# The chain from the reloaded attention rows to the FFN in two halves of 256 rows, BN_AGGR for mean and variance, and a new order

## The chip, the cores and the metric

The kernel runs on one core of a Trainium2 chip. The metric is device time in microseconds (us) of one execution. Engines: PE is TensorE's matmuls, PEld its weight loads, DVE is VectorE, ACT is ScalarE, POOL is GpSimd, SP is SyncE, which issues the DMAs.

## What is computed

A block of attention and a block of FFN, each between layer norms, over x of 4 x 1024 x 512 in float32.

```python
x = L0_attn_x
x = x + _layernorm(_L0_attn_ref(_layernorm(x), ...))
x = x + _layernorm(_L0_ffn_ref(_layernorm(x), ...))

def _L0_attn_ref(x, qkv_w, conv_w0, conv_b0, conv_w1, conv_b1, proj_w, proj_b, ln_w, ln_b):
    tok = x.reshape(B, H * W // C, C)              # tokens of 16 channels
    qkv = (tok @ qkv_w).reshape(B, -1, 3, C)
    ...                                            # two branches, windows of 8 tokens: softmax(q k) v + a 3x3 conv of v
    att = jnp.concatenate([x1, x2], axis=-1) @ proj_w + proj_b
    mu = att.mean(-1, keepdims=True)
    var = ((att - mu) ** 2).mean(-1, keepdims=True)
    tok = tok + (att - mu) * lax.rsqrt(var + EPS) * ln_w + ln_b
    return jnp.transpose(tok, (0, 2, 1)).reshape(B, H, W)

def _L0_ffn_ref(x, w_gate, w_up, w_down, s_gate, s_up, s_down):
    gate = jax.nn.silu((x @ w_gate) * s_gate)      # 512 x 2048, int8 weights
    up = (x @ w_up) * s_up
    return ((gate * up) @ w_down) * s_down         # 2048 x 512
```

## The kernel before

The 4096 rows are worked in 8 tiles of 512. All engines walk one list of named steps, and each engine has code for the steps that concern it, so that an engine's queue is the list cut down to its own steps. `BEFORE` is the preamble: the attention of tile 0 and most of the first half of tile 1's, the casts of the int8 weights, and the chain to the FFN of tile 0. Then comes one body per tile. A body has 48 slots: for each of 16 chunks m a `gate`, an `up` and a `down` slot, three chunks apart for `down` (LAG), and a table (`STEADY`, for the last tile but one `ENDING`) says after which slot each attention or norm step stands. Tile t's body holds the FFN of tile t, the second half of the attention of tile t+1 (p and a in the table) and the first half of that of tile t+2 (b and c); group 0 of a tile is p or b, group 1 is a or c. `STEADY` runs for tiles 0 to 5 (1 to 4 in a hardware loop), `ENDING` for tile 6, `STEADY` once more for tile 7.

The steps of the attention: `ln1_stats`, `ln1_fin`, `ln1_apply` (the first layer norm), `xt` (transposes of normalised rows, TensorE, copied by ScalarE), `qkv` (projection), `qx` (ScalarE copies q into PSUM `ps_x`), `qk` and `pv` (VectorE multiplies 128x2048 products into `prod`, GpSimd halves them into `sum4`), `qk_sum` and `pv_sum` (VectorE reduces), `softmax`, `exp`, `recip`, `attn_out` (GpSimd, in one case of the preamble VectorE), `cat` (transposes), `proj`, `square`, `cent_var`, `cent_std`, `cent_out` (the inner norm; GpSimd scales by `lnw` and adds the tokens into `ratt`). A bank `ps_w[0]` or `ps_w[1]` is handed from one TensorE step to the next once ScalarE or VectorE has read it.

The chain to the FFN: `att_store` (SyncE) writes `ratt` to memory in two parts and reloads it in another layout as `o1` (in the trace, `o`), 2 x 256 rows. `ffn_norm1` (VectorE) takes BN_STATS of the four 128-row blocks of `o1` and `mean_var` makes mean and variance of them with six small operations; GpSimd's `inv_std` makes the inverse deviation (add, power, multiply); `norm1_add` scales `o1` (ScalarE) and adds it to `xr` (VectorE); `ffn_norm2` does the statistics of `xr`, `norm2_apply` (ScalarE) writes the normalised rows into `o1`; `fx` (t, hi, u) transposes them (TensorE), ScalarE rounds them to f16 as `xhi` and VectorE writes the rest as `xlo`. `gate` of chunk 0 waits for the lower 256 rows, `gate` of chunk 8 for the upper ones. `keep_x1` frees `xr` for `load_xr` of the next tile. `finish`, `finish_apply` and `finish_add` are the last norm. In front of the first gate stand matmuls on `ident` without a use for their result (`warm`, `warm_cat`, `warm_fx`).

Of the kernel before, what the change touches and what calls it, by code (L numbers as in the profile page):

```python
# [7 lines left out]
P = 128  # L8
B, H, W = 4, 1024, 512
C = 16  # L10
# [42 lines left out]
def sandwich_kernel(nc, x, qkv_w, conv_w0, conv_b0, conv_w1, conv_b1, proj_w, proj_b, ln_w, ln_b,  # L53
                    w_gate, w_up, w_down, s_gate, s_up, s_down, scratch, out):
    with ExitStack() as ctx:  # L55
# [25 lines left out]
        epsx = sb("epsx", [P, NQ])  # L81
# [128 lines left out]
        f_chain = sem("f_chain")  # L210
        f_stats = sem("f_stats")
        f_pool = sem("f_pool")
        f_rs = sem("f_rs")
# [67 lines left out]
        def body_steps(plan, last=False):  # L281
# [14 lines left out]
            if last:  # L296
# [1101 lines left out]
```

## Time and profile before

| | |
|---|---|
| time, median of 3 runs | 1010.31 us (1009.2 to 1011.27) |
| the profiled execution | 1010.6 us |
| its span, first to last instruction | 1008.9 us |
| PE busy | 909.3 us, 90% of the span |
| DVE busy | 852.0 us, 84% |
| POOL busy | 720.0 us, 71% |
| ACT busy | 624.6 us, 62% |
| mean granted clock of TensorE | 0.959 |
| DMA | 46.14 MB, 46 GB/s on the mean |

The busy time is a mean over stages. The time before the first gate matmul and the bodies have to be read apart. An idle time is put down to the engine whose signal came last. Instructions can overlap: a group's duration may reach beyond the start of the next on the same engine.

### The profile page before, as it was taken

What the parts mean: (1) busy time and instruction counts of PE and PEld (TensorE: products, weight loads), DVE (VectorE), ACT (ScalarE), POOL (GpSimd) and SP (SyncE); (2) the same over time, 40 slices, a digit from 0 to 9 for tenths busy, and PEclk for the clock granted to TensorE, in tenths of its full rate; (3) what the DMA queues carried; (4) which work ended last, traced back from release to release, by engine and by line L of the source; (5) the groups of instructions that cost most, each with busy time, mean ns of one, the idle gap of its engine ahead of it and who ended that gap; (6) DMA issues with size and microseconds to landing.
All of it is one profiled execution on the core that took longest, in us unless ns stands there. A gap on an engine that the chain in (4) does not pass through costs nothing. (4 is left out here: it accounts for less than half of the span.)

```text
span 1008.9 us, 18469 instructions
## 1 busy us (share of the span) xinstructions
PE 909.3 (90%) x6503; PEld 707.5 (70%) x6503; DVE 852.0 (84%) x1270; ACT 624.6 (62%) x1058; POOL 720.0 (71%) x539
## 2 busy tenths in 40 slices
PE   3636628999999999999999999999999999999996
PEld 3424418777777777877777777777787777777773
DVE  6898898899999999999999999999999999353132
ACT  2745826867586767766686758676776665452431
POOL 3656656787779886997789876987699788542332
PEclk9866958999999999999999999999999999999998
DMA  6011050014102320114002310232011301120001
GB/s 179 0 43 42 1 125 1 1 42 114 34 2 64 84 64 0 33 48 111 16 0 62 98 48 0 62 83 62 1 25 53 76 17 63 54 52 2 22 1 42
DMA packets 78319, 46.14 MB, mean 46 GB/s; under 512 B 39608, under 2 KB 72376, under 8 KB 78264
## 3 DMA queue, kind: packets, MB, share of 16 engines
q1 hardware_dynamic: 73400, 45.10, 16.9%
q10 hardware_dynamic: 4864, 0.32, 0.3%
q8 instruction: 33, 0.54, 0.2%
q14 instruction: 22, 0.18, 0.1%
HBM read 28.63 MB, written 16.78 MB: 45 GB/s over the span
## 5 line engine op out<-in xcount | busy, mean ns | idle before, releaser
L1118 DVE TENSOR_TENSOR prod<-ps_x,qkvl 128x2048 f32<-128x2048 f32 x128 | 290.8, 2280 | 10.4 <-ACT ps_x L786 6.5
L650 PE MATMUL ps_gate<-xhi,wg 128*128 128x256 f16 x1024 | 230.6, 273 | 2.3 <-DVE xlo L1229 1.7
L650 PE MATMUL ps_gate<-xlo,wg 128*128 128x256 f16 x1024 | 230.5, 273 | 0.0
L650 PE MATMUL ps_up<-xhi,wu 128*128 128x256 f16 x1024 | 230.5, 273 | 0.0
L650 PE MATMUL ps_up<-xlo,wu 128*128 128x256 f16 x1024 | 230.5, 273 | 0.0
L856 ACT ACTIVATE gact<-ps_gate,sgate 128x256 f32<-128x256 f32 x256 | 106.6, 467 | 157.0 <-PE ps_gate L650 155.4
L1012 POOL TENSOR_TENSOR flo<-fuse,fhi 128x512 f16<-128x512 f32 x128 | 148.4, 1162 | 72.4 <-ACT fhi L862 72.3
L952 POOL TENSOR_TENSOR sum<-prod 128x1024 f32<-128x1024 f32 x64 | 150.6, 2364 | 39.9 <-DVE prod L1118 36.9
L1238 DVE SCALAR_TENSOR_TENSOR fuse<-ps_up,sup,gact 128x256 f32<-128x256 f32 x256 | 110.3, 472 | 75.8 <-PE ps_up L650 63.9
L961 POOL TENSOR_TENSOR sum<-prod 128x1024 f32<-128x1024 f32 x64 | 151.5, 2369 | 19.5 <-DVE prod L1118 12.8
L670 PE MATMUL ps_acc<-wd,flo 128*128 128x512 f16 x512 | 153.3, 379 | 0.0
L670 PE MATMUL ps_acc<-wd,fhi 128*128 128x512 f16 x512 | 153.3, 379 | 0.0
L606 PE MATMUL ps_w<-wqkvl,xt 128*128 128x256 f32 x512 | 135.6, 404 | 18.5 <-ACT xt L768 12.7
L606 PEld LDWEIGHTS ps_w<-wqkvl,xt 128*128 128x128 f32 x512 | 97.9, 202 | 40.1 <-ACT xt L768 16.1
L650 PEld LDWEIGHTS ps_gate<-xhi,wg 128*128 128x128 f16 x1024 | 100.2, 98 | 22.1 <-DVE xlo L1229 1.9
L650 PEld LDWEIGHTS ps_gate<-xlo,wg 128*128 128x128 f16 x1024 | 100.2, 98 | 21.1
L650 PEld LDWEIGHTS ps_up<-xlo,wu 128*128 128x128 f16 x1024 | 100.2, 98 | 13.5
L650 PEld LDWEIGHTS ps_up<-xhi,wu 128*128 128x128 f16 x1024 | 100.7, 98 | 11.6
L777 ACT ACTIVATE qkvl<-ps_w 128x512 f32<-128x512 f32 x128 | 74.8, 595 | 44.3 <-PE ps_w L606 40.5
L670 PEld LDWEIGHTS ps_acc<-wd,flo 128*128 128x128 f16 x512 | 50.1, 98 | 60.4
L1127 DVE TENSOR_REDUCE ps_x<-sum 128x256 f32<-128x1024 f32 x64 | 78.0, 1220 | 15.6 <-POOL sum L952 15.6
L862 ACT ACTIVATE fhi<-fuse 128x512 f16<-128x512 f32 x128 | 80.3, 628 | 1.3 <-DVE fuse L1238 1.3
(155 smaller groups left out, 1411.4 us busy)
## 6 DMA issues: line engine op xcount, KB each, us to landing
xb<-in_L_attn_x SPq DMA_DIRECT2D x64, 128.0 KB, 2.7
xr<-in_L_attn_x SPq DMA_DIRECT2D x16, 512.0 KB
attn_rows<-ratt SPq DMA_DIRECT2D x16, 512.0 KB, 3.5
o<-attn_rows SPq DMA_DIRECT2D x32, 256.0 KB, 4.2
out_x<-y SPq DMA_DIRECT2D x15, 512.0 KB
x<-in_L_ffn_w_gate SPq DMA_DIRECT2D x1, 1024.0 KB, 5.4
xr<-in_L_ffn_w_up SPq DMA_DIRECT2D x1, 1024.0 KB, 8.2
out_x<-y SPq DMA_DIRECT2D x2, 256.0 KB
```

The source lines that it names most:

```text
L606: mm = nc.tensor.matmul(bank.ps[:, 4 * WC * i:4 * WC * i + 4 * WC], xt[:, 2 * wp + i, :], wqkvl[:, br].rearrange("p f x -> p (f x)"), star ...
L650: mm = nc.tensor.matmul(ps[:, HALF * i:HALF * i + HALF], w[:, k, P * j:P * j + P], xs[:, k, rows], start=(k == 0 and part == 0), stop=(k = ...
L670: return nc.tensor.matmul(ps_acc[q][:], f[:, m % SPLITS, HALF * i + P * q:HALF * i + P * q + P], wd[:, 2 * c + i, :], start=(c == 0 and pa ...
L777: nc.scalar.activation(qkvl[:, g, br, :, 2 * wp:2 * wp + 2].rearrange("p f w x -> p w f x"), bank.ps[:].rearrange("p (w f x) -> p w f x", ...
L856: a = nc.scalar.activation(gact[:, m % 2, part], ps_gate[:, part], ACT.Silu, scale=sgate[:, j:j + 1])
L862: nc.scalar.activation(fhi[:, m % SPLITS, :], fuse[:, m % 2, :], ACT.Copy).then_inc(fhi_done, 1)
L952: nc.gpsimd.tensor_tensor(dst.rearrange("p (s c) -> p s c", c=4), s[:, :, 0:4], s[:, :, 4:8], ALU.add).then_inc(half_done, 1)
L961: nc.gpsimd.tensor_tensor(dst.rearrange("p (s j) -> p s j", j=4), s[:, :, 0:4], s[:, :, 4:8], ALU.add).then_inc(half_done, 1)
L1012: nc.gpsimd.tensor_tensor(flo[:, m % SPLITS, :], fuse[:, m % 2, :], fhi[:, m % SPLITS, :], ALU.subtract).then_inc(flo_done, 1)
L1118: nc.vector.tensor_tensor(prod[:, half].rearrange("p (s j k) -> p s j k", j=WIN, k=WIN), left[:, :, None, :].broadcast_to([P, 4 * WIN, WIN ...
L1127: nc.vector.tensor_reduce(dst, sum4[:, u % 2, :].rearrange("p (s c) -> p s c", c=4), AX.X, ALU.add).then_inc(sum_done, 1)
L1238: a = nc.vector.scalar_tensor_tensor(fuse[:, m % 2, part], ps_up[:, part], sup[:, j:j + 1], gact[:, m % 2, part], ALU.mult, ALU.mult)
```

## The change

The chain from `o1` to `fx` is cut in two: `ffn_norm1`, `norm1_add`, `ffn_norm2` and `norm2_apply` now have a step for each 256 rows, with semaphores of their own. Mean and variance come from BN_AGGR (`moments`, with one spare small operation between the wait and the first BN_AGGR), which gives the variance and the mean with its sign, so GpSimd's `row_std` has one operation more, and for the second norm two more. `ln1_stats` keeps `mean_var`. The multiplication by `lnw` is split in two so that the first half of the rows of `ratt` is ready before the second. `keep_x1` also waits for the last addition into `xr`. All three tables are new; `START` is empty and its steps stand in `BEFORE`.

```diff
-        def scale_norm(eng):
-            eng.tensor_tensor(cent[:].rearrange("p h t c -> p (h t) c"), cent[:].rearrange("p h t c -> p (h t) c"),
-                              lnw[:, None, :].broadcast_to([P, WIN * WIN, C]), ALU.mult).then_inc(lnw_chain, 1)
...
+        def scale_and_add(eng, queue, n, g):
...
             for hi in range(2):
                 c = slice(HB * hi, HB * hi + HB)
+                eng.tensor_tensor(rows[:, :, c], rows[:, :, c], lnw[:, None, c].broadcast_to([P, WIN * WIN, HB]),
+                                  ALU.mult).then_inc(lnw_chain, 1)
+                queue.wait_ge(lnw_chain, 2 * n + hi + 1)
                 eng.tensor_tensor(ratt[:, c, :, WIN * g:WIN * g + WIN].rearrange("p c h t -> p h t c"),
                                   cent[:, :, :, c], token[:, :, :, c], ALU.add).then_inc(ratt_done, 1)
...
+            def row_std(rs, nb, mean, var, chain, base, done, scale=None):
+
+                n = rs.shape[1]
+                nc.gpsimd.tensor_tensor(nb, mean, (negx if scale else negone)[:, 0:n], ALU.mult).then_inc(chain, 1)
+                nc.gpsimd.tensor_tensor(rs, var, eps1[:, 0:n], ALU.add).then_inc(chain, 1)
+                pool.wait_ge(chain, base + 2)
+                nc.gpsimd.tensor_tensor(rs, rs, neghalf[:, 0:n], ALU.pow).then_inc(chain, 1)
+                pool.wait_ge(chain, base + 3)
+                a = nc.gpsimd.tensor_tensor(nb, nb, rs, ALU.mult)
+                if scale:
+                    a = nc.gpsimd.tensor_tensor(rs, rs, scale[:, 0:n], ALU.mult)
+                a.then_inc(done, 1)
...
+            def moments(i, rows, st, chain, n, done):
+
+                dve.wait_ge(chain, n)
+                nc.vector.tensor_scalar(spare[:], st[:, rows[0], 1:2], 0.5, None, ALU.mult)
+                for q in rows:
+                    a = nc.vector.bn_aggr(fmv[:, i, q, :], st[:, q, :])
+                a.then_inc(done, 1)
...
+            def ffn_norm1(t, hi, bank):
+
+                dve.wait_ge(s_o1[hi], 32 * (t + 1))
+                row_stats(o1, 0, (2 * hi, 2 * hi + 1), fst, n1_chain, 2 * t + hi + 1, n1_stats)
...
-            def ffn_norm2(t, bank):
-                dve.wait_ge(xr_sum, NQ * t + NQ)
-                row_stats(xr, 1, fst, f_chain, 6 * t + 3, f_stats, XSCALE ** -2)
+            def ffn_norm2(t, hi, bank):
+                dve.wait_ge(xr_sum, NQ * t + 2 * hi + 2)
+                row_stats(xr, 1, (2 * hi, 2 * hi + 1), fst, n2_chain, 2 * t + hi + 1, n2_stats)
...
-                  (35, ("pv_sum", b, 1)), (35, ("token_bias", c)), (35, ("ffn_norm1", 1)), (36, ("pv_sum", b, 2)),
...
-                  (43, ("ffn_norm2", 1)), (43, ("pv_sum", b, 3)), (43, ("attn_out", b)), (44, ("qk", c, 0)),
...
+                  (35, ("ffn_norm1", 1, 0)), (35, ("finish_apply", 0, 0)), (36, ("qkv", c, 0, 2)), (36, ("recip", b)),
...
+                  (42, ("norm2_apply", 1, 0)), (42, ("qkv", c, 1, 2)), (43, ("attn_out", b)), (43, ("pv_sum", b, 2)),
```

In the steady table the slots are: `ffn_norm1` 35, now 35 and 37; `norm1_add` 38, now 38 and 40; `ffn_norm2` 43, now 41 and 46; `norm2_apply` 44, now 42 and slot 2 of the next body; `fx` of the lower half 46, now 44, of the upper half 4 and 8, now 3 and 8; `attn_out` of a 19, now 22, and its `cat` 23, now 24; `load_xr` 22, now 0; `load_xb` 33, now 22; `att_store` 24, now 21. What follows are the queues of single engines, one row per instruction or per run of like ones (a call that takes two passes over float32 is one row here and two records in the trace).

TensorE's queue from the last projection steps of the preamble to the first gate matmul. L724 (now L733) are the matmuls without a use, L640 (L649) the transposes of `fx`, L617 (L626) `cat` of the next tile. Before:

```order
48 L606 MATMUL ps_w<-wqkvl,xt 128x256 x4
49 L724 MATMUL ps_acc<-ident 128x128 x16
50 L640 MATMUL ps_w<-ident,o 128x128 x8
51 L617 MATMUL ps_w<-ident,qkvl 128x128 x4
52 L650 MATMUL ps_gate<-xhi,wg 128x256
```

and now:

```order
47 L733 MATMUL ps_acc<-ident 128x128 x8
48 L615 MATMUL ps_w<-wqkvl,xt 128x256 x4
49 L607 MATMUL ps_w<-ident,xb 128x128 x4
50 L615 MATMUL ps_w<-wqkvl,xt 128x256 x6
51 L649 MATMUL ps_w<-ident,o 128x128 x8
52 L733 MATMUL ps_acc<-ident 128x128 x8
53 L626 MATMUL ps_w<-ident,qkvl 128x128 x4
54 L659 MATMUL ps_gate<-xhi,wg 128x256
```

One of the two warming groups went ahead of the projection steps, the other behind the transposes.

VectorE's queue in the same place, from the additions into `xr` on. L1127 (L1151) is a reduction, L1118 (L1142) a product, L1229 (L1255) writes `xlo`. Before:

```order
147 L1220 TENSOR_TENSOR xr<-o,xr 128x512 x4
148 L1197 BN_STATS fst<-xr 128x6 x4
149 L1071 TENSOR_TENSOR fmv<-fst 128x4
150 L1072 TENSOR_TENSOR fst<-fst 128x4
151 L1073 TENSOR_TENSOR fst<-fst 128x4
152 L1075 TENSOR_SCALAR fmv<-fmv 128x4
153 L1076 SCALAR_TENSOR_TENSOR fst<-fst 128x4
154 L1079 SCALAR_TENSOR_TENSOR fmv<-fst 128x4
155 L1127 TENSOR_REDUCE attn<-sum 128x256
156 L1118 TENSOR_TENSOR prod<-ps_x,qkvl 128x2048 x2
157 L1229 TENSOR_TENSOR xlo<-ps_w,xhi 128x2x256 x2
```

and now:

```order
146 L1246 TENSOR_TENSOR xr<-o,xr 128x512 x4
147 L1227 BN_STATS fst<-xr 128x6 x2
148 L1220 TENSOR_SCALAR spare<-fst 128x1
149 L1222 BN_AGGR fmv<-fst 128x2 x2
150 L1151 TENSOR_REDUCE attn<-sum 128x256
151 L1142 TENSOR_TENSOR prod<-ps_x,qkvl 128x2048
152 L1255 TENSOR_TENSOR xlo<-ps_w,xhi 128x2x256 x2
153 L1227 BN_STATS fst<-xr 128x6 x2
154 L1220 TENSOR_SCALAR spare<-fst 128x1
155 L1222 BN_AGGR fmv<-fst 128x2 x2
156 L1142 TENSOR_TENSOR prod<-ps_x,qkvl 128x2048
```

One product and the statistics of the upper 256 rows went behind `xlo`.

TensorE's queue where the last transposes of tile 0 stand (the second row of four transposes, L598, now L607; L606, now L615, are the projection steps); the load of tile 1's rows waits for these transposes. Before:

```order
18 L606 MATMUL ps_w<-wqkvl,xt 128x256 x2
19 L598 MATMUL ps_w<-ident,xb 128x128 x4
20 L606 MATMUL ps_w<-wqkvl,xt 128x256 x4
21 L598 MATMUL ps_w<-ident,xb 128x128 x4
22 L606 MATMUL ps_w<-wqkvl,xt 128x256 x8
23 L583 MATMUL ps_w<-mv,pair 128x16
```

and now:

```order
18 L615 MATMUL ps_w<-wqkvl,xt 128x256 x4
19 L607 MATMUL ps_w<-ident,xb 128x128 x4
20 L615 MATMUL ps_w<-wqkvl,xt 128x256 x4
21 L607 MATMUL ps_w<-ident,xb 128x128 x4
22 L615 MATMUL ps_w<-wqkvl,xt 128x256 x4
23 L592 MATMUL ps_w<-mv,pair 128x16
```

Two of the four projection steps of the last branch now stand ahead of its second four transposes.

## Rows read from the trace of the kernel before

**Rows 1.** Busy time by stage: stretch, length, then each engine's us (instructions), PEclk, DMA, GB/s.

```profile
28.46:161.72 133.26, 64.25 (x267) 49.00 (x267) 124.17 (x128) 73.32 (x101) 83.87 (x47) 0.72 0.15 40
267.27:377.02 109.75, 109.34 (x808) 85.79 (x806) 104.03 (x151) 77.09 (x132) 90.61 (x66) 1.00 0.19 49
815.55:909.47 93.92, 91.57 (x708) 70.10 (x706) 64.68 (x109) 50.48 (x90) 62.27 (x50) 1.00 0.17 46
```

**Rows 2.** Waits of TensorE, 161.7 to 998 us: us in total, times, longest.

```profile
PE ps_gate L650 <- DVE xlo L1229: 1.7, 1, 1.7
PE ps_w L617 <- POOL qkvl L459: 1.7, 4, 0.4
PE ps_w L627 <- ACT catt L798: 0.6, 1, 0.6
PE ps_gate L650 <- ACT gact L856: 0.6, 1, 0.6
PE ps_w L598 <- ACT xb L761: 0.4, 1, 0.4
```

**Rows 3.** VectorE in order of time, end of the preamble: start, us, what, count.

```profile
139.09 2.28 DVE L1118 TENSOR_TENSOR prod<-ps_x,qkvl 128x2048 f32<-128x2048 f32 x1
141.28 2.46 DVE L1206 BATCH_NORM_STATS2 fst<-o 128x6 f32<-128x512 f32 x4
...
152.12 0.17 DVE L1071 TENSOR_TENSOR fmv<-fst 128x4 f32<-128x4 f32 x1
152.20 0.16 DVE L1072 TENSOR_TENSOR fst<-fst 128x4 f32<-128x4 f32 x1
...
152.47 0.17 DVE L1075 TENSOR_SCALAR fmv<-fmv 128x4 f32<-128x4 f32 x1
...
152.82 1.21 DVE L1127 TENSOR_REDUCE attn<-sum 128x256 f32<-128x1024 f32 x1
...
160.29 1.29 DVE L1229 TENSOR_TENSOR xlo<-ps_w,xhi 128x512 f16<-128x512 f32 x2 [1.86 <-ACT xhi L828]
```

**Rows 4.** Waits of VectorE, 28 to 162 us: us in total, times, longest.

```profile
DVE prod L1118 <- ACT ps_x L786: 6.5, 2, 3.5
DVE prod L1118 <- POOL sum L952: 2.4, 1, 2.4
DVE xlo L1229 <- ACT xhi L828: 1.9, 1, 1.9
DVE xr L1220 <- ACT o L817: 0.5, 1, 0.5
DVE ps_x L1127 <- POOL sum L952: 0.3, 1, 0.3
```

**Rows 5.** TensorE in order of time in the preamble, with the idle time before.

```profile
51.27 1.09 PE L598 MATMUL ps_w<-ident,xb 128*128 128x128 f32 x4 [0.97 <-ACT qkvl L777]
...
152.96 6.23 PE L724 MATMUL ps_acc<-ident 128*128 128x128 f32 x32 [11.01 <-DVE fmv L1079]
159.02 1.04 PE L640 MATMUL ps_w<-ident,o 128*128 128x128 f32 x8
...
161.72 0.27 PE L650 MATMUL ps_gate<-xhi,wg 128*128 128x256 f16 x1
```

**Rows 6.** SyncE's DMA queue, the load of tile 1's rows.

```profile
52.39 6.10 SPq L498 DMA_DIRECT2D xb<-in_L_attn_x  x8
```

**Rows 7.** ScalarE in order of time in the preamble: a cast, and the second norm applied.

```profile
57.15 1.90 ACT L847 ACTIVATE wu<-xr 128x2048 f16<-128x2048 int8 x1
...
154.58 2.93 ACT L823 ACTIVATE o<-xr,frs 128x512 f32<-128x512 f32 x4 [5.77 <-POOL frs L919]
```

**Rows 8.** GpSimd in order of time, the power on two columns, in a body.

```profile
352.18 0.71 POOL L917 TENSOR_TENSOR frs<-frs,neghalf 128x2 f32<-128x2 f32 x1
```

**Rows 9.** VectorE and GpSimd in order of time, behind the last down matmul.

```profile
1000.48 0.16 DVE L1071 TENSOR_TENSOR fmv<-yst 128x1 f32<-128x1 f32 x1
...
1001.31 0.58 POOL L915 TENSOR_TENSOR frs<-fmv,eps 128x1 f32<-128x1 f32 x1 [1.43 <-DVE fmv L1079]
```

More of the change, by code:

```diff
@@ L80, in sandwich_kernel @@
         eps1 = sb("eps1", [P, WIN])
-        epsx = sb("epsx", [P, NQ])
+        negone = sb("negone", [P, NQ])
+        negx = sb("negx", [P, NQ])
+        xscale = sb("xscale", [P, NQ])
+        spare = sb("spare", [P, 1])
         epsc = sb("epsc", [P, 1])
@@ L1189, in cent_out, with row_stats, ffn_norm1, norm1_add @@
                     dve.wait_ge(cn_done, n + 1)
-                    scale_norm(nc.vector)
-                    dve.wait_ge(lnw_chain, n + 1)
                     dve.wait_ge(xl_done, 4 * n + 4)
-                    add_token(nc.vector, g)
-            def row_stats(src, i, st, chain, base, done, scale=1.0, blocks=slice(0, NQ)):
-                for q in range(blocks.start, blocks.stop):
+                    scale_and_add(nc.vector, dve, n, g)
+            def moments(i, rows, st, chain, n, done):
[4 more added lines that the diff above has]
+                a.then_inc(done, 1)
+            def row_stats(src, i, rows, st, chain, n, done):
+                for q in rows:
                     a = nc.vector.bn_stats(st[:, q, :], src[:, q, :])
                 a.then_inc(chain, 1)
-                mean_var(st[:, blocks], W, fmv[:, i, blocks, 0], fmv[:, i, blocks, 1], chain, base, done, -1.0, scale)
-            def ffn_norm1(t, bank):
-                for hi in range(2):
-                    dve.wait_ge(s_o1[hi], 32 * (t + 1))
-                    for q in (2 * hi, 2 * hi + 1):
-                        a = nc.vector.bn_stats(fst[:, q, :], o1[:, q, :])
-                a.then_inc(f_chain, 1)
-                mean_var(fst, W, fmv[:, 0, :, 0], fmv[:, 0, :, 1], f_chain, 6 * t, f_stats, -1.0)
-            def norm1_add(t, bank):
+                moments(i, rows, st, chain, n, done)
+            def ffn_norm1(t, hi, bank):
+                dve.wait_ge(s_o1[hi], 32 * (t + 1))
+                row_stats(o1, 0, (2 * hi, 2 * hi + 1), fst, n1_chain, 2 * t + hi + 1, n1_stats)
+            def norm1_add(t, hi, bank):
                 dve.wait_ge(s_xr, 32 * t + 32)
-                for q in range(NQ):
+                for q in (2 * hi, 2 * hi + 1):
                     dve.wait_ge(o1_scaled, NQ * t + q + 1)
@@ L1261, in finish @@
                 dve.wait_ge(acc_read, NQ * t + 2 * hi + 2)
-                row_stats(y, 2, yst, y_chain, 3 * (2 * t + hi), y_stats, blocks=slice(0, 2))
+                row_stats(y, 2, range(2), yst, y_chain, 2 * t + hi + 1, y_stats)
             nc.vector.memset(ones[:], 1.0).then_inc(wvt_done, 1)
```

250 lines of the change are left out of this document (129 added, 121 removed).

## The prediction

> **What bounds the kernel now.** I read the shares by engine first, then the busy time by stage, then the waits of TensorE and VectorE, and last the queues in order of time around the places that the change touches. TensorE is busy 90% of the span (the table above), but that mean mixes two stages. From 28.46 us to the first gate matmul at 161.72 us TensorE works 64.25 of 133.26 us and VectorE 124.17 [rows 1]: the preamble ends when VectorE and the chain behind it let the first FFN half go. From there TensorE is packed: one pass of the body (267.27 to 377.02) has 109.34 of 109.75 us of matmuls, and VectorE, second, 104.03. The waits of TensorE between 161.7 and 998 us confirm it: 1.7, 1.7, 0.6, 0.6 and a last one of 0.4, together 5.0 us out of 836 [rows 2]. The work that TensorE has behind the first gate is the same in both kernels, so the time after the change is the sum of three things: when the first gate starts, how many of those 5.0 us of waits remain or are added, and the tail behind the last down matmul. All sums are made against the profiled execution, 1010.6 us (span 1008.9), which stands 0.3 us above the median of the runs shown, 1010.31.
>
> **Part 1: the work of VectorE in the preamble.** The steps ahead of the first `xlo` lose one product (`qk` of window group c, unit 1, is now behind it): 139.09 to 141.28, 2.2 us [rows 3]. `ffn_norm2` of the upper 256 rows is behind it too: two of four BN_STATS of 0.62, 1.2 us. The two `mean_var` blocks go: each runs from the first small operation at 152.12 to 152.82, 0.7 us, together 1.4 us. In their place stand three `moments` blocks (one spare operation, two BN_AGGR each). No row shows a BN_AGGR. The nearest from below are the small operations on 128x4 values, 0.16 to 0.17 us long, 0.08 apart without a wait (152.12, 152.20) and 0.2 with one (from 152.20 to 152.47 stand one of each) [rows 3]; the nearest from above is a BN_STATS itself, 0.62. An aggregation reads six numbers, so I take the lower row: a block is 0.1 of wait and three times 0.08, about 0.35 us, three make 1.05. Splitting the multiplication by `lnw` adds about 0.1. Sum: 2.2 + 1.2 + 1.4 - 1.05 - 0.1, so 3.7 us less work.
>
> Here a rule of the Trainium skill speaks against counting so. The rows show small operations that start 0.08 us apart although each lasts 0.16, and 0.2 apart where there is a wait. The page "VectorE: DVE Perf Modes", section "The DRAIN you can't avoid", says that the next operation does not start until the pipe is empty and that a semaphore between two costs nothing extra. By it, as an estimate by that page with the durations of the rows, a block of six would cost about 1.0 us and one of three 0.5, and two of the first for three of the second would save 0.5 us; by the rows they save 0.35. The trace disagrees on both halves of the rule, and its spacing is what I use.
>
> **Part 2: the waits of VectorE in the preamble.** Before, it waits 8.1 us between its first product and the last `xlo`: 3.0 (the other half of the 6.5 lies ahead of that product), 2.4, 1.9, 0.5 and 0.3 [rows 4]. The new order moves them. (a) The load of the next tile's rows is issued when the last transpose of tile 0 is done. Before, that transpose stood ahead of the four projection steps, at 51.27, and the load went out at 52.39 [rows 5, 6]. Now it stands behind two of them, and its bank is free only when ScalarE has copied the second. ScalarE reaches that copy after an exponential (ready near 50), a cast of 1.90 us and five copies of 0.6 [rows 7], with two cold projection steps between: near 58. The eight loads, 6.1 us to issue and 2.7 to land, are in near 67; VectorE wants them at 65. A new wait of 2.0 us. (b) The two waits for ScalarE's `ps_x` copies of tile 1 (3.0, and the 2.4 that stood behind GpSimd) remain: the first shrinks to about 0.9 because VectorE comes later, the second grows to between 2.4 and 4.1, since the transposes of the attention output now stand between projection steps 1 and 2 of that branch and wait for VectorE's own `attn_out`; I take 4.1, as TensorE has idled by then and runs at the lower clock. (c) The end of the chain: with the FFN rows in halves, TensorE can transpose the lower half after two of ScalarE's applications, which it could before as well; the wait for `xhi` stays at 2.0. With 0.2 for the later `scale_pow2` the sum is 0.2 + 2.0 + 0.9 + 4.1 + 2.0, about 9.2 us against 8.1. So VectorE is done with the last `xlo` 3.7 - 1.1 = 2.6 us earlier, at 158.9 instead of 161.5.
>
> **Part 3: TensorE's queue ahead of the gate.** Before, 32 warming matmuls (16 calls, two records each) run from 152.96 for 6.2 us, and the transposes start at 159.02 only because these are in front: the first two applications, half of the 2.93 us of four [rows 7], were ready at 156.1. Now one warming group is far ahead and the other, 16 records, stands behind the transposes. The transposes start when VectorE's statistics of the lower half, GpSimd's five small operations (the power on two columns is 0.71 [rows 8], the whole about 1.6) and two applications (1.4) are through: about 155.4 by the walk above. TensorE is cold by then: eight transposes 1.8 to 2.0 us (four took 1.09 at 51.27, eight 1.04 at 159.02), sixteen warming records 1.8 to 3.5 (half of the 6.2 us row and about what is left of it at the upper level), `cat` 0.5. The first gate starts between 159.5 and 161.4; I take 160.0, 1.7 us earlier. The granted clock of that stretch was 0.72 on the mean [rows 1], that is, between its two levels 1.2 and 2.4 GHz. So the warming group, not `xlo`, is last there, and it eats 1 us of the gain.
>
> **Part 4: the body.** The cover of every edit in it is TensorE's packed queue; what can be lost is lost only where VectorE, GpSimd or ScalarE comes late to it. VectorE: four `mean_var` of 0.7 to 0.8 go (3.1 us), six `moments` of 0.35 come (2.1): 104.0 becomes 103.0. GpSimd: four chains of three become six of four or five, 90.6 plus about 3; neither reaches 109.3. In order of slots: `fx` moves from slot 46 to 44, so that 6.6 us of TensorE's work lie between it and the next gate instead of 3.1, and its own input, `norm2_apply` of two rows, must be ready two slots earlier; the chain for it starts two slots earlier and is half as long. Laying VectorE's queue against TensorE's slots with the same durations leaves 1.0 us there, but only 0.2 to 0.5 us at two fuse steps: in a pass without waits TensorE starts the `up` of chunk 11 at 77.4 us, and the fuse of chunk 10 is done at 76.9; from there VectorE has `finish` 3.0, a reduction 1.1, a sum 0.6, a product 2.2 and the next fuse 0.8, done at 84.6, where the `up` of chunk 12 wants it at 84.8. The transposes of `cat` move one slot back while `attn_out` moves three back; its 0.4 us wait in each of four passes stays or goes. SyncE: `load_xr` now stands ahead of the output store and waits for `keep_x1`; the store is queued behind it, some 20 us before `y` is wanted again. The load of `xb` moves ahead eleven slots but behind the reloads, and lands over 15 us early. Both cost nothing. Sum for the body: 0, with a lower bound of -3.3 (all the waits of [rows 2] but the 1.7 on `xlo` go) and an upper of +1.2 in each of six passes.
>
> In the last pass with attention (815.55 to 909.47) the chain to the last tile's first gate ends late: `xlo` holds TensorE for 1.7 us, the largest wait in [rows 2]. Now the lower half goes through in front of the upper, and by the same walk `xlo` is ready 3 us before the gate, although `cent_out` comes some 4 us later in that pass. The 1.7 us go.
>
> **Part 5: the tail.** `mean_var` on one column takes from 1000.48 to GpSimd's start at 1001.31, 0.8 us [rows 9]; now 0.35 plus 0.1 for GpSimd's fourth operation. 0.4 us less.
>
> **Sum:** 1.7 + 0 + 1.7 + 0.4 = 3.8 us. 1010.6 - 3.8 = 1006.8 in the profiled execution, 1006.5 as a median.
>
> **The rivals.** (A) *VectorE becomes the bound of the body.* It works 104 of 109.8 us and its other 5.5 are mostly waits for GpSimd, which its queue order makes. If a BN_AGGR costs 0.4 us instead of 0.08 (it would have to be closer to BN_STATS' 0.62 than to a small operation), the six blocks cost 6 us instead of 2.1, VectorE needs 107, and with its waits 109.4 is passed; or the 0.2 us left at slot 35 isn't there. Either gives about 1.2 us in each of six passes: 1006.5 + 7, 1013.5. It decides from a block cost of about 0.9 us, or from 0.2 us of lateness. For it speaks the thin slack, against it that a wait of TensorE gives VectorE time to catch up. (B) *Nothing comes of the preamble.* If the load of the next tile's rows and the cold projection steps cost 2 us more than I gave them, and the last pass gains but the body gives back its 1.7, the result is 1009.5: within 0.2%. (C) *The waits of the preamble vanish.* If the 2.0 and 4.1 us of part 2 don't show (ScalarE's queue keeps up and TensorE is warm), the first gate starts near 155.5 and the time is 1002.
>
> **How the numbers follow.** Forecast 0.55 (1004 to 1009), A 0.17, B 0.18, C 0.10. A change of 0.2%, 2 us, is about what a measurement of this kernel can tell from none. The forecast lies on the faster side of 1008.3 in nine of ten of its cases: faster 0.50 + 0.10 = 0.60; same 0.05 + 0.18 and 0.01 of A, 0.24; slower 0.16. The range runs from 1002.0 (C) to 1012.0, which leaves out the worse half of A and the better half of C.
>
> **What would show it.** The first gate matmul near 160, with warming matmuls right ahead of it; a wait of VectorE on the BN_STATS of `xb` near 65 us; BN_AGGR rows of 0.16 us; no wait of TensorE on `xlo` at the last tile; waits of TensorE in a body pass of at most 0.5 us. A gate later than 161.5, passes longer than 110.5 us, or BN_AGGR of 0.4 us would prove the forecast wrong.

## The result

The changed kernel takes 1013.76 us in the median (1012.49 to 1015.58), 1.0037 times the kernel before, with a 95% interval of 1.0028 to 1.0047. That is 3.4 us slower, where 3.8 us faster was forecast, and above the upper end of the range, 1012.0. The profiled execution took 1013.88 us, its span is 1011.8.

Busy time of each engine in the kernel after, from its profile page:

```profile
PE 913.4 (90%) x6503; PEld 708.9 (70%) x6503; DVE 840.3 (83%) x1218; ACT 621.4 (61%) x1060; POOL 748.4 (74%) x669
```

VectorE has 12 us less to do than before, GpSimd 28 us more, and neither decides. Busy time by stage, in the columns of [rows 1]: preamble, a steady pass, the pass of `ENDING`:

```profile
28.46:162.09 133.63, 67.75 (x270) 52.66 (x271) 122.74 (x128) 72.66 (x100) 87.29 (x58) 0.69 0.15 40
268.15:378.96 110.81, 109.73 (x807) 85.48 (x806) 103.54 (x146) 76.19 (x132) 94.33 (x82) 1.00 0.18 49
821.35:912.51 91.16, 91.16 (x705) 69.90 (x704) 64.45 (x102) 52.56 (x91) 62.79 (x68) 1.00 0.18 47
```

With the start of each tile's first gate matmul the time splits with no more than rounding left over (the last tile of before begins at 909.24; the window in [rows 1] was drawn a little further):

| | before | after | difference |
|---|---|---|---|
| start to first gate | 161.72 | 162.09 | +0.37 |
| pass 0 | 105.55 | 106.06 | +0.51 |
| passes 1 to 5 | 548.28 | 553.20 | +4.92 |
| pass 6 (`ENDING`) | 93.69 | 91.16 | -2.53 |
| pass 7, to the last down matmul | 89.75 | 89.74 | 0.0 |
| tail | 9.9 | 9.6 | -0.3 |
| span | 1008.9 | 1011.8 | +2.9 |

The loss stands in the steady passes. TensorE's waits from 161.9 to 1002 us, to be laid beside [rows 2]:

```profile
PE ps_w L649 <- ACT qkvl L786: 5.7, 12, 0.6
PE ps_up L659 <- DVE fuse L1264: 0.2, 1, 0.2
```

All waits of before are gone, the 1.7 us on `xlo` and the four on `cat` among them. In their place stand twelve at L649, the transposes of `fx`, two in each of six passes. In order of time in one pass, TensorE:

```profile
365.86 1.03 PE L615 MATMUL ps_w<-wqkvl,xt 128*128 128x256 f32 x4
...
370.63 0.59 PE L679 MATMUL ps_acc<-wd,flo 128*128 128x512 f16 x2
371.81 0.66 PE L649 MATMUL ps_w<-ident,o 128*128 128x128 f32 x4 [0.59 <-ACT qkvl L786]
372.81 0.66 PE L649 MATMUL ps_w<-ident,o 128*128 128x128 f32 x4 [0.35 <-ACT qkvl L786]
```

The idle time is counted from the modelled end of a matmul. What a wait costs is read from start to start: two down matmuls are passed on in 0.43 us, so the first transposes could have started at 371.06 and are 0.75 late; the second come 1.00 behind the first, where four transposes need 0.44: 0.56 late. Together 1.31 us a pass, for 0.94 of idle time. The pass of before that had no wait in the list took 109.22 us; with 1.31 that is 110.53, and the passes of after take 110.6. The `cat` wait of before, 0.4 us of idle, cost 0.5 in the same way (109.75).

That 110.53 comes so close is in part chance, for there is one more loss that the list is too coarse to show. The matmuls of a projection step are passed on in 0.86 us where nothing waits (365.86 to 366.72). In front of the `up` of chunk 12 it is 1.15, so that `up` starts 0.29 us late, with 0.13 us of idle time put down to VectorE's fuse; it is so in each of passes 1 to 5:

```profile
573.27 1.03 PE L615 MATMUL ps_w<-wqkvl,xt 128*128 128x256 f32 x4
574.42 0.28 PE L659 MATMUL ps_up<-xhi,wu 128*128 128x256 f16 x1
```

The 109.22 us of before hold small delays too, 0.2 us together, at other places. ScalarE in the same stretch:

```profile
369.76 1.52 ACT L832 ACTIVATE o<-xr,frs 128x512 f32<-128x512 f32 x2 [2.86 <-POOL frs L946]
371.18 0.58 ACT L786 ACTIVATE qkvl<-ps_w 128x512 f32<-128x512 f32 x1
371.66 0.62 ACT L871 ACTIVATE fhi<-fuse 128x512 f16<-128x512 f32 x1
372.18 0.58 ACT L786 ACTIVATE qkvl<-ps_w 128x512 f32<-128x512 f32 x1
```

`norm2_apply` (L832) stands ahead of the copies of two projection steps, the first of which TensorE had finished near 366.9 (its four matmuls from 365.86). ScalarE waits 2.86 us for GpSimd's inverse deviation with that copy behind it, and the two banks that `fx` is to use stay full. GpSimd is late because VectorE's statistics are done only at 366.9; GpSimd is then on a long addition that lasts to 367.1, a `flo` stands next in its queue, and the five small operations start behind that:

```profile
366.66 0.24 DVE L1222 BATCH_NORM_AGGREGATE fmv<-fst 128x2 f32<-128x6 f32 x2
```

```profile
367.05 1.17 POOL L1036 TENSOR_TENSOR flo<-fuse,fhi 128x512 f16<-128x512 f32 x1
368.16 0.20 POOL L939 TENSOR_TENSOR frs<-fmv,negx 128x2 f32<-128x2 f32 x1
...
369.52 0.20 POOL L946 TENSOR_TENSOR frs<-frs,xscale 128x2 f32<-128x2 f32 x1
```

In the preamble, VectorE's waits from 28 to 165 us are in the main those that the forecast named, the load of `xb` among them:

```profile
DVE prod L1142 <- ACT ps_x L795: 9.6, 3, 4.7
DVE bst L1109 <- DMA xb<-in_L_attn_x: 2.1, 1, 2.1
DVE xlo L1255 <- ACT xhi L837: 1.9, 2, 1.7
```

The 9.6 are 4.68 ahead of the first product, then 0.86 and 4.07. TensorE in order of time at the end of the preamble, as in [rows 5]:

```profile
156.38 1.97 PE L649 MATMUL ps_w<-ident,o 128*128 128x128 f32 x8 [11.37 <-ACT o L832]
158.14 3.62 PE L733 MATMUL ps_acc<-ident 128*128 128x128 f32 x16
161.55 0.70 PE L626 MATMUL ps_w<-ident,qkvl 128*128 128x128 f32 x4
162.09 0.27 PE L659 MATMUL ps_gate<-xhi,wg 128*128 128x256 f16 x1
```

The last `xlo` is done at 159.70, 1.9 us earlier than before (161.58), and the gate does not see it: the warming group runs for 3.62 us at a granted clock of 0.50, the lower of the two levels, in front of `cat` and the gate. The two halves of that stretch, granted clock third from the end:

```profile
158.14:160.00 1.86, 1.86 (x10) 1.86 (x10) 1.68 (x3) 0.60 (x1) 1.86 (x2) 0.50 0.00 0
160.00:161.76 1.76, 1.76 (x10) 1.76 (x9) 1.73 (x6) 0.00 (x0) 1.76 (x3) 0.50 0.03 9
```

### The profile page after: what moved, and what is told of

Same layout as the page of the kernel before. It is cut to its first block, busy times and chain, and to the rows that moved or that the text cites. A ratio compares the mean times of both kernels' runs of the same rounds, so it can differ in the third digit from the quotient of the medians.

```text
span 1011.8 us, 18543 instructions
## 1 busy us (share of the span) xinstructions
PE 913.4 (90%) x6503; PEld 708.9 (70%) x6503; DVE 840.3 (83%) x1218; ACT 621.4 (61%) x1060; POOL 748.4 (74%) x669
## 4 chain that ended last, share of the span: by engine, by line
PE 60%; POOL 13%; DVE 12%; issue 7%; ACT 6%; SPq 1%; DMA 1%; POOLq 0%; ACTq 0%; DVEq 0%
PE ps_gate L659 16%; PE ps_acc L679 15%; PE ps_up L659 15%; PE ps_w L615 5%; DVE prod L1142 5%; POOL sum L984 4%; PE ps_w L639 2%; POOL flo L1036 2%; POOL ratt L492 2%; PE ps_w L607 2%; POOL cent L489 1%; POOL frs L942 1%; PE ps_w L626 1%; PE ps_w L649 1%; DVE ps_x L1151 1%
## 5 line engine op out<-in xcount | busy, mean ns | idle before, releaser
L1142 DVE TENSOR_TENSOR prod<-ps_x,qkvl 128x2048 f32<-128x2048 f32 x128 | 289.8, 2280 | 17.8 <-ACT ps_x L795 17.7
L1036 POOL TENSOR_TENSOR flo<-fuse,fhi 128x512 f16<-128x512 f32 x128 | 151.3, 1182 | 63.4 <-ACT fhi L871 63.4
L615 PE MATMUL ps_w<-wqkvl,xt 128*128 128x256 f32 x512 | 138.7, 410 | 21.1 <-ACT xt L777 19.6
L615 PEld LDWEIGHTS ps_w<-wqkvl,xt 128*128 128x128 f32 x512 | 100.0, 206 | 40.7 <-ACT xt L777 22.1
L1151 DVE TENSOR_REDUCE attn<-sum 128x256 f32<-128x1024 f32 x64 | 76.4, 1201 | 1.9 <-POOL sum L984 1.9
```

The source lines that it names most:

```text
L615: mm = nc.tensor.matmul(bank.ps[:, 4 * WC * i:4 * WC * i + 4 * WC], xt[:, 2 * wp + i, :], wqkvl[:, br].rearrange("p f x -> p (f x)"), star ...
L1036: nc.gpsimd.tensor_tensor(flo[:, m % SPLITS, :], fuse[:, m % 2, :], fhi[:, m % SPLITS, :], ALU.subtract).then_inc(flo_done, 1)
L1142: nc.vector.tensor_tensor(prod[:, half].rearrange("p (s j k) -> p s j k", j=WIN, k=WIN), left[:, :, None, :].broadcast_to([P, 4 * WIN, WIN ...
L1151: nc.vector.tensor_reduce(dst, sum4[:, u % 2, :].rearrange("p (s c) -> p s c", c=4), AX.X, ALU.add).then_inc(sum_done, 1)
```

## The experiments

The theory after the result: the change loses 1.3 us in each steady pass to the order of ScalarE's queue and the lateness of the chain in front of it, more than the waits were worth that it takes away, and in the preamble the warming group eats what VectorE gained. Rivals: the new instructions cost it (BN_AGGR, GpSimd's longer chains), or VectorE bounds the pass (rival A of the prediction). All kernels are made from the kernel after. In the diffs stand neighbouring steps of the tables, as they follow one another.

The starts of executions differ: VectorE's first product came between 27.60 and 29.76 us in kernels whose queues are nearly alike up to there. For the preamble I count from that product to the first gate; it is 133.26 us before and 133.14 after.

**The old order with the new code.** The tables are those of before, each halved step twice in its slot.

```diff
-(35, ("ffn_norm1", 1, 0)),
-(42, ("norm2_apply", 1, 0)),
-(44, ("fx", 1, 0, 0)), (44, ("fx", 1, 0, 1)),
...
+(35, ("ffn_norm1", 1, 0)), (35, ("ffn_norm1", 1, 1)),
+(44, ("norm2_apply", 1, 0)), (44, ("norm2_apply", 1, 1)),
+(46, ("fx", 1, 0, 0)), (46, ("fx", 1, 0, 1)),
```

> The code of the kernel after (halves, BN_AGGR, GpSimd's longer chains, lnw in two parts) with the four tables of the kernel before, the two halves of each step standing next to each other in the old step's slot; the group of warming matmuls waits for both halves' statistics. Theory (the loss is the order alone): passes of 109.75 us as before, the first gate at 161.3 to 161.8, the tail 0.4 us shorter, 1009.5 to 1010.2. Rival (the instructions themselves cost it, above all GpSimd's six chains of four and five operations or VectorE's waits in the aggregation): passes of 110.3 or more, 1013 or more.

Measured: 1010.06 us, ratio 0.9996 (0.9987 to 1.0006). The first pass takes 105.86 us (before 105.55), passes 1 to 4 take 109.49 to 109.69, where before has 109.74 to 109.80, the preamble 132.97 us. The waits of TensorE at `cat` in passes 1 to 4, here L629, have shrunk from 0.4 to 0.16 us of idle:

```profile
431.34 1.09 PE L629 MATMUL ps_w<-ident,qkvl 128*128 128x128 f32 x8 [0.16 <-POOL qkvl L472]
...
908.48 0.28 PE L662 MATMUL ps_gate<-xhi,wg 128*128 128x256 f16 x1 [1.72 <-DVE xlo L1258]
```

So the code costs nothing that can be measured in this order; the 1.72 us at the last tile, which the order of after removes, are back. The loss is the order's.

**ScalarE's queue alone.** Nothing moves on another engine.

```diff
-(42, ("norm2_apply", 1, 0)), (42, ("qkv", c, 1, 2)),
+(42, ("qkv", c, 1, 2)), (42, ("norm2_apply", 1, 0)),
```

> The kernel after with only ScalarE's queue changed in the steady body: the second norm of two rows stands behind the copy of projection step 2 of the last branch, not ahead of it; nothing moves on any other engine. Theory (the copy that waits behind the norm is what holds the bank): the copy of step 2 is done near 367.5 instead of 371.8 and the first transposes start about 371.35, the second 371.95, where 371.81 and 372.81 were; a pass is 0.8 us shorter, six give 4.8 us, 1009. Rival (the norm itself, by GpSimd's inverse deviation at 369.7, is what is late): the transposes start no earlier than 371.7 and a pass keeps at least 110.4 us, under 1.5 us in all.

Measured: 1010.58 us, 3.2 us less than after; passes of 110.12. The transposes of one pass:

```profile
371.03 0.65 PE L649 MATMUL ps_w<-ident,o 128*128 128x128 f32 x4 [0.16 <-ACT o L832]
371.96 0.65 PE L649 MATMUL ps_w<-ident,o 128*128 128x128 f32 x4 [0.27 <-ACT qkvl L786]
```

One copy out of the norm's shadow gives 0.46 us a pass, not the 0.8 expected: the first transposes now wait for the norm itself, and the second still for the second copy, which `fhi` (0.61 us) comes before. ScalarE's order is 0.5 of the 1.3 us; neither the theory's 109.8 nor the rival's 110.4 came out.

**The chain one step earlier.** VectorE's statistics stand ahead of a fuse, and GpSimd's small operations ahead of the `flo`; TensorE's and ScalarE's queues are as in after.

```diff
-(40, ("pv_sum", b, 1)), (41, ("ffn_norm2", 1, 0)),
+(40, ("pv_sum", b, 1)), (40, ("ffn_norm2", 1, 0)),
```

> The kernel after with the second norm's statistics of the lower rows at slot 40 of the steady body instead of 41: on VectorE they stand ahead of the fuse of chunk 13, on GpSimd the inverse deviation stands ahead of a flo of 1.17 us; ScalarE's and TensorE's queues are unchanged. Theory (the chain to the transposes is late by VectorE's and GpSimd's queues, and ScalarE's copies stand behind it): the inverse deviation is done at 368.6 instead of 369.7, the copies by 371.4, the waits at the two transposes fall from 0.6 and 0.35 to under 0.2 together, against a new wait of up to 0.3 us at the up of chunk 14; a pass takes 109.5 to 109.8, the whole 1007 to 1009. Rival (the copies of the projections take that long in any case): passes of 110.4 or more.

Measured: 1008.93 us, 4.8 us less than after, ratio to before 0.9991 (0.9982 to 1.0001); passes of 109.94 us, a little over the 109.8 given. ScalarE waits 1.71 instead of 2.86 us for the inverse deviation, and no wait at `fx` is left. GpSimd and ScalarE in one pass:

```profile
365.14 0.20 POOL L939 TENSOR_TENSOR frs<-fmv,negx 128x2 f32<-128x2 f32 x1
...
366.66 1.16 POOL L1036 TENSOR_TENSOR flo<-fuse,fhi 128x512 f16<-128x512 f32 x1
```

```profile
366.74 1.52 ACT L832 ACTIVATE o<-xr,frs 128x512 f32<-128x512 f32 x2 [1.71 <-POOL frs L946]
```

TensorE, waits from 161.9 us on:

```profile
PE ps_w L626 <- POOL qkvl L469: 1.0, 4, 0.3
```

This is not the `cat` wait of before. That one stood at slot 23, 55 us into a pass, and is gone in every kernel with the new order. This one stands at slot 45, 106 us into the pass, where TensorE now comes earlier; in after the wait at `fx` in front had hidden it. In before, and in this kernel:

```profile
321.94 0.54 PE L617 MATMUL ps_w<-ident,qkvl 128*128 128x128 f32 x3 [0.41 <-POOL qkvl L459]
```

```profile
372.45 0.65 PE L626 MATMUL ps_w<-ident,qkvl 128*128 128x128 f32 x4 [0.26 <-POOL qkvl L469]
```

The new wait at the `up` of chunk 14 that was expected came too: it starts 0.2 us later than in after, measured from the pass's first gate. The two remedies don't add: with both (the kernel with all together, below) a pass takes 109.93 us, as with this one alone. Once the chain is early, the order on ScalarE costs nothing.

**`fx` two slots later**, where before has it, once with `cat` left at 45 and once with `cat` at 47.

```diff
-(44, ("fx", 1, 0, 0)), (44, ("fx", 1, 0, 1)), (45, ("cat", b, 0)),
+(45, ("cat", b, 0)), (46, ("fx", 1, 0, 0)), (46, ("fx", 1, 0, 1)),
```

> The kernel after with the transposes of the next tile's lower rows at slot 46 of the steady body instead of 44 (behind cat), where the kernel before has them. Theory (in the six steady passes they come before ScalarE has copied the projections that stand behind the second norm in its queue): the twelve waits of 0.35 to 0.65 us go, a pass takes 109.3 to 109.5 us instead of 110.6, six passes give 7 us back, 1006.8. Rival 1 (the chain is simply late): the wait comes back at the first gate of the next tile on xlo, 0.5 to 1 us a pass, and the gain is under 2 us. Rival 2 (VectorE bounds the body): passes stay at 110.6 and the waits turn up at the fuse steps.

> The kernel after with fx at slot 46 and cat at slot 47 of the steady body, both where the kernel before has them (with fx alone moved a pass took 111.87 us: cat, now in front, waited 1.3 us for GpSimd's addition, and the upper fx 0.8 for VectorE). Theory (these 1.3 us are cat standing one slot behind its input, nothing of fx): cat's wait goes, a pass takes 109.3 to 110.3. Rival (whatever chain stands there, the attention output of this order ends too late for the end of the pass): the wait stays over 0.5 us and passes over 110.6.

Measured: 1021.32 us with `fx` alone, 1012.59 with both. My theory of the first fell: the waits at `fx` went, but passes took 111.87 us. The waits of TensorE in it, and in the second kernel:

```profile
PE ps_w L626 <- POOL qkvl L469: 8.6, 7, 1.4
PE ps_w L649 <- DVE ln L1123: 4.0, 5, 0.9
```

```profile
PE ps_w L649 <- DVE ln L1123: 4.9, 5, 1.0
```

With `cat` one slot further back its wait is gone from the steady passes and a pass takes 110.42 us, just outside the 109.3 to 110.3 of the theory and under the rival's bound. What is left is a wait of the upper half's transposes, in the next pass, for VectorE to have read the bank of the first norm. In the kernel after TensorE arrives there 1.3 us later against VectorE's work, by the delay at `fx`; that this is what hides the wait is argued, not tried. The first pass, which has no such wait yet, is the shortest of all kernels (104.66 us, 1.4 less than in after), but the pass of `ENDING` takes 92.88 us, 1.7 more than in after, and gives that back. Whether it is `xlo` at slot 46 that holds VectorE up into the next pass was not tried apart. A later transpose gained 0.2 us a steady pass in this order, where an earlier chain gained 0.65.

**VectorE made to work more.** Each block of one spare operation and two BN_AGGR is done four times.

```diff
+                for k in range(4):
+                    nc.vector.tensor_scalar(spare[:, k:k + 1], st[:, rows[0], 1:2], 0.5, None, ALU.mult)
+                for k in range(3):
+                    for j, q in enumerate(rows):
+                        nc.vector.bn_aggr(extra[:, 2 * k + j, :], st[:, q, :])
```

> The kernel after with every block of three small operations behind the statistics (one spare, two BN_AGGR) done four times, into tiles of their own: 12 operations 0.08 us apart instead of 3, 0.7 us more for each of the six blocks of a pass, 4.3 us more of VectorE's 110.6, as if a BN_AGGR cost 0.4 us. Theory (a pass is set by TensorE and by the chain to the transposes, not by VectorE's total): only the blocks on that chain count, the lower half's norm 2 in full and at most one of norm 1, a pass grows by 0.7 to 1.4 us, and the added wait stands at the same transposes of fx. Rival A (VectorE is the bound): a pass grows by 3.5 us or more, and TensorE waits for the fuse steps.

Measured: 1018.38 us. A pass takes 111.14 us, 0.56 more than 110.58. VectorE in the chain of that kernel:

```profile
366.92 0.34 DVE L1222 TENSOR_SCALAR spare<-fst 128x1 f32<-128x1 f32 x4
367.18 0.50 DVE L1225 BATCH_NORM_AGGREGATE extra<-fst 128x2 f32<-128x6 f32 x6
367.60 0.21 DVE L1227 BATCH_NORM_AGGREGATE fmv<-fst 128x2 f32<-128x6 f32 x2
```

A block takes 0.81 us from its start to the next operation's (367.73), 0.58 more than in after, so VectorE had 3.5 us more in a pass, and five sixths of it cost nothing. The span grew by 3.7 us in all (1015.5): 3.0 in the six steady passes, 0.8 in pass 6, 0.3 in the tail, less 0.4 in the preamble. Rival A wanted 3.5 in every pass; the theory's 0.7 to 1.4 was too much as well. Its place was wrong besides: measured from the pass's first gate, the `up` of chunk 4 starts 0.2 us later than in after and that of chunk 12 another 0.24, both behind a fuse, where rival A had the waits, and only the last 0.1 is at the transposes of `fx` (5.7 us of idle in all became 6.3). The idle time at the `up` of chunk 12 went from 0.13 to 0.36 us. So VectorE's total is no bound, but at that one fuse it has no slack left, in after already.

**The warming group**, ahead of `fx` as before, and left out.

```diff
-("fx", 0, 0, 0), ("load_xr", 0), ("fx", 0, 0, 1), ("ffn_norm2", 0, 1), ("warm_fx", 0),
+("warm_fx", 0), ("fx", 0, 0, 0), ("load_xr", 0), ("fx", 0, 0, 1), ("ffn_norm2", 0, 1),
```

> The kernel after with one step moved in the preamble: the 16 warming matmul records stand ahead of the transposes of the first FFN rows, as in the kernel before, instead of behind them. Theory (the warming group holds the first gate): it runs in TensorE's idle time from 153.2 to about 156.8, the transposes follow at 156.7, and the first gate comes 2.7 us behind them, as before (159.02 to 161.72): near 159.4 instead of 162.09, and the whole time falls by about 2.7 us, to 1011. Rival 1 (the warming behind the transposes pays for itself by the clock): the granted clock falls in the gap, the first gates run at the lower level and the time stays within 0.5 us of 1013.8. Rival 2 (xlo, not the group, is last): the gate moves by under 1 us.

> The kernel after without the 16 warming matmul records between the transposes of the first FFN rows and cat. Theory (the group holds the gate): cat follows GpSimd's addition, which ends at 159.25, and the first gate is at 159.8 instead of 162.09. What is bought with the group is the clock: if TensorE then runs at the lower level for the first microseconds, a chunk of 5 to 6.5 us costs up to twice as much and the gain of 2.3 is used up, whole time 1013 to 1014. Rival (the clock is at the upper level with the transposes and cat alone): 1011.5.

Measured: 1012.79 us with the group ahead, 1013.17 without one. From the first product to the first gate it is 131.38 and 131.77 us, 1.8 and 1.4 less than after. In both `cat` waits for GpSimd's addition. With the group ahead:

```profile
152.56 3.78 PE L734 MATMUL ps_acc<-ident 128*128 128x128 f32 x16 [9.18 <-DVE fmv L1223]
156.13 1.22 PE L650 MATMUL ps_w<-ident,o 128*128 128x128 f32 x8
158.66 0.66 PE L627 MATMUL ps_w<-ident,qkvl 128*128 128x128 f32 x4 [1.31 <-POOL qkvl L470]
```

The first gate came at 159.16, 2.9 us earlier than in after, of which 1.2 is the earlier start of that execution; that the expectation of 2.7 looks met is chance. The first pass then took 0.70 us more (106.76): its first chunk waits 0.46 us for VectorE's first-norm statistics. 1.0 us is left. Without a group the first pass takes 1.70 us more, for TensorE's clock is low at its start, where in after the granted clock is 1.00 from 161.76 us on:

```profile
159.00:162.00 3.00, 3.00 (x15) 2.28 (x15) 2.97 (x7) 0.60 (x1) 2.92 (x4) 0.50 0.00 0
162.00:165.00 3.00, 3.00 (x22) 2.57 (x20) 3.00 (x8) 1.61 (x2) 2.50 (x4) 0.76 0.02 5
165.00:168.00 3.00, 3.00 (x29) 2.67 (x28) 2.13 (x10) 3.00 (x7) 0.32 (x1) 1.00 0.00 0
```

So the group's place is worth about 1 us at most; the best of the three is in TensorE's idle time, ahead of the transposes, though its 0.4 us over no group at all lie within the scatter of the runs.

**The two waits of the preamble**, on top of the group ahead.

```diff
-("xt", a, 1, 0), ("qkv", a, 1, 0),
-("cast", 0, 6), ("xt", a, 1, 1), ("qkv", a, 1, 2),
+("xt", a, 1, 0), ("xt", a, 1, 1), ("qkv", a, 1, 0),
+("cast", 0, 6), ("qkv", a, 1, 2),
...
-("cat", a, 0), ("qkv", b, 1, 2), ("qkv", b, 1, 3), ("pv_sum", a, 2), ("cat", a, 1), ("qx", b, 1),
+("qkv", b, 1, 2), ("qkv", b, 1, 3), ("pv_sum", a, 2), ("qx", b, 1), ("cat", a, 0), ("cat", a, 1),
```

> The kernel with the warming group ahead of the transposes (gate at 159.16), and two moves in the preamble: the last transposes of tile 0 ahead of the three projection steps that stood in front of them, and cat of the second group behind the projection steps of the next branch. Theory (VectorE's waits of 2.1 on the load of xb and of 4.1 on ps_x are made by these two places, and VectorE's queue sets the end of the preamble): both go or shrink to under 1 us in all, the first gate comes at 154 to 157, and the time falls to 1007 to 1009. Rival (other engines are as late as VectorE there: GpSimd's attention output, ScalarE's casts): the waits turn up at other lines and the gate stays within 1 us of 159.2.

Measured: 1008.66 us, 4.1 less than with the group alone; first product to gate 126.94 us, 4.4 less; the first gate at 154.77. VectorE's waits in order of time:

```profile
93.38 2.29 DVE L1143 TENSOR_TENSOR prod<-ps_x,qkvl 128x2048 f32<-128x2048 f32 x1 [0.32 <-ACT ps_x L796]
111.55 1.23 DVE L1152 TENSOR_REDUCE ps_x<-sum 128x256 f32<-128x1024 f32 x1 [2.59 <-POOL sum L976]
```

The load's 2.1 us are gone whole, and the 4.07 gave way to 2.59 for GpSimd: both answers hold, each in part. A wait of 0.32 us for `ps_x` stays of the 0.86.

**All together, and `cat` one slot later.** The last but one of these also moved the statistics of tile 2 ahead of VectorE's last product of the preamble, the last does not.

```diff
-(45, ("cat", b, 0)),
+(46, ("cat", b, 0)),
```

> All of it together: the warming group ahead, the two moves in the preamble, the statistics at slot 40, and the second norm behind the copy of projection step 2 on ScalarE. If the losses are separate, as the theory has them: the gate of the preamble kernel, passes of 109.2 to 109.7, 1001 to 1003. Rival (a wait that is taken away comes back at VectorE, the next engine): passes stay above 110 and the whole is above 1005.

> The last kernel (all changes together, 1004.4) with two more moves: cat of the next tile at slot 46 of the steady body instead of 45, and, in the preamble, the first norm's statistics of tile 2 ahead of VectorE's last product instead of behind it. Theory: cat's wait for GpSimd's addition (0.26 us, 0.5 from start to start) goes in six passes, passes take 109.3 to 109.5 instead of 109.93; the wait of 0.59 on mv in the first chunk goes and that chunk takes 6.5 instead of 7.3 us; 1000.5 to 1001.5. Rival (what takes a wait's place is the next step of the same queues: cat later makes the inner norm's chain later, the product later makes softmax later): passes stay at 109.7 or more, and the whole within 1 us of 1004.4.

> All changes together (1004.4) with cat of the next tile at slot 46 instead of 45 alone, without the move of the statistics in the preamble, which made the first pass 0.9 us longer. Theory (the two moves of the last kernel are separate): passes of 109.44 us as there, the first pass 105.7 to 106.2, the whole 0.9 us below that kernel's 1003.26: 1002.4, counted from equal starts. Rival (the longer first pass came with cat at slot 46): first pass near 107, 1003.3.

| | median | ratio to before | first product to gate | first pass | steady pass |
|---|---|---|---|---|---|
| all together | 1004.37 | 0.9949 (0.9933 to 0.9966) | 126.90 | 106.15 | 109.93 |
| `cat` at 46, statistics moved | 1003.26 | 0.9924 (0.9911 to 0.9938) | 127.53 | 107.03 | 109.44 |
| `cat` at 46 | 1001.55 | 0.9909 (0.9896 to 0.9923) | 127.44 | 105.71 | 109.44 |

The first is 1.4 us above what was expected: what stands at `cat` (0.26 us of idle, 0.5 in time) was not in my sum. `cat` at 46 takes just that away. Moving the statistics cost 1.3 us in the first pass instead of gaining 0.8: in place of the wait of 0.59 on `mv` came one of 1.53 for the rest of the first norm and one of 0.49 at a fuse behind it, since the product of 2.3 us now stands between that norm's statistics and its last small operations:

```profile
167.22 0.63 PE L650 MATMUL ps_w<-ident,o 128*128 128x128 f32 x4 [1.53 <-DVE ln L1124]
```

The last kernel beats both: 9.2 us, 0.9%, less than before measured beside it, 12.2 less than after. Behind the first gate TensorE has only two waits over 0.2 us in it, 0.59 and 0.43 us:

```profile
162.97 0.40 PE L593 MATMUL ps_w<-mv,pair 128*128 128x16 f32 x2 [0.59 <-DVE mv L1104]
...
856.44 0.65 PE L627 MATMUL ps_w<-ident,qkvl 128*128 128x128 f32 x4 [0.43 <-POOL qkvl L470]
```

## Why the prediction was wrong

**Part 1 held.** VectorE's work from its first product to the last `xlo` is 124.0 us before and 120.4 after, 3.65 less against 3.7. A BN_AGGR is 0.15 to 0.17 us long and 0.07 apart from the next; a block takes 0.22 us (142.88 to 143.10), where 0.35 was taken; three blocks are 0.4 us less than counted, and that the sum fits all the same is in that part luck. The rows' spacing was the right measure. The Trainium skill, page "VectorE: DVE Perf Modes", section "The DRAIN you can't avoid", has the next operation start only when the pipe is empty, and adds that one which is not held starts earlier. The operations of a block, 0.15 us long and 0.07 apart, go with the addition, which the prediction left out. The section's other half, that a semaphore between two operations costs nothing extra, this case's rows do not bear out: 0.08 us apart without a wait, 0.2 with one [rows 3].

**Part 2 held** in the terms that it had: 2.10 for 2.0 on the load, issued at 59.69 where ScalarE's copy was put near 58, 0.86 for 0.9 and 4.07 for 4.1 on `ps_x`, 1.9 for 2.0 at `xlo`. But the last `xlo` is 1.9 us earlier, not 2.6: the start slipped by 0.49 us instead of 0.2, and the waits of 0.3 on `xr` and 0.3 on `ps_x`, which stayed, stood in the 8.1 of before and not in the 9.2 of after.

**Part 3 failed by its size.** The mechanism was right (the group, not `xlo`, is last), but I set 160.0 with 161.4 as the upper end, and it is 162.09. The transposes started at 156.38 instead of 155.4, and the sixteen records took 3.62 us, just over the dearer end of my 1.8 to 3.5, since TensorE was at the lower clock level the whole time. Of the 1.7 us that the sum had here nothing came; +0.37 did.

**Part 4 failed in its step, and this decided.** It laid VectorE's queue against TensorE's slots and found 1.0 us of room at `fx`. ScalarE's queue was not laid there, though the order of the steps has it: `norm2_apply` at slot 42 is the new place of a waiting instruction, and two copies stand behind it. Nor was GpSimd's `flo` in front of the five operations. The sum had 0 with an upper bound of +1.2 a pass; it was +0.5 in the first and about +1.0 in each of the others, 5.4 us in all. The upper bound held for the sum, 7.2; one pass, pass 5, went over it by 0.2. What the lower bound counted on did come: the waits of [rows 2] in passes 0 to 4 went. The four on `cat` stand 55 us into a pass, where TensorE isn't late in after, and they are gone as well in the kernels that have no wait at `fx`; it is the new order that took them. So a pass gained 0.5 us there and 0.2 in small delays, and lost 1.3 at `fx` and 0.3 at the `up` of chunk 12. The last of these is a place that part 4 had named, with 0.2 us of room.

**The last attention pass and the tail held.** The 1.7 us at the last tile went, the 0.6 on `catt` with them (2.5 us shorter), and the tail is 0.3 shorter against 0.4.

**The rivals.** A named the right time, 1013.5, with a wrong mechanism: it had VectorE as the bound, by a dear BN_AGGR or a late fuse at slot 35. BN_AGGR is as cheap as the forecast had it, and the kernel with the blocks four times as dear shows that a pass grows by 0.56 us where VectorE has 3.5 more. The late fuse is there, but costs 0.3 us a pass, not 1.2. That its time came out is luck. B, nothing of the preamble, was right as far as the gate goes, but had the body at 1.7 us where it was 5.4. C, the waits of the preamble gone, became true only when they were taken out by hand: that was worth 4.4 us. The signs were well chosen: a gate later than 161.5 us and passes longer than 110.5 us were to prove the forecast wrong, and both came.

## What to carry over

Where a step is cut in halves or moved earlier, lay the queue of each engine that carries part of it, and for each wait in it name what stands behind: a copy that frees a bank holds TensorE there just as the step itself does. A wait that goes can uncover the next one on the same engine, so a gain is counted to the next wait and not further; and two waits on the same tile and line need not be the same wait, so look where in a pass each stands. Idle time behind a matmul understates a wait; the distance from start to start, against the same rows without a wait, gives its price.

## What was not expected of the hardware

In the last three kernels, whose queues are the same up to there, VectorE's first product came at 27.60, 29.76 and 28.43 us. 2 us, 0.2% of the time, are made or lost before the first product, and a preamble is better compared from there than from the start.

The sixteen warming records took 3.62 us in after and 3.03 us in the kernel with the statistics at slot 40, with the same queue in front of them:

```profile
157.91 3.03 PE L733 MATMUL ps_acc<-ident 128*128 128x128 f32 x16
```

```profile
156.00:159.00 3.00, 2.85 (x14) 2.85 (x15) 1.13 (x3) 1.78 (x4) 2.92 (x3) 0.50 0.00 0
159.00:161.30 2.30, 2.30 (x17) 2.29 (x17) 2.27 (x7) 0.00 (x0) 2.30 (x2) 0.74 0.03 7
```

The granted clock rose within the group in this execution (0.74 from 159.00 on) and behind it in the other (0.50 to 161.76), so between these two executions the group, and the first gate behind it, differ by about 0.6 us.
